# An unread identity matmul in every step of layer 1, and one head-sum per two steps in layer 0, in a two-layer graph attention kernel

## What is computed

```python
# layer 0 (transformer): K[src], Q[dst], V[src]
score = einsum('ehd,ehd->eh', K[src], Q[dst]) / sqrt(32) + edge_bias
ex = exp(score - segment_max(score, dst)[dst])
out = segment_sum(ex / segment_sum(ex, dst)[dst] * V[src], dst) @ Wp + bp   # then layer norms and an FFN
# layer 1 (GAT): feat = (h @ W_lin + b_lin) @ W_gat; el, er = sums of feat * attn_l, feat * attn_r per head
e = leaky_relu(el[src] + er[dst], 0.2)
out = segment_sum(softmax over dst of e * feat[src], dst)                   # then a bias, leaky_relu, h_in + out
```

## Time and profile before

| | us |
|---|---|
| median of 3 runs (5990.07 to 6003.05) | 5992.57 |
| the profiled execution | 5990.54 |
| its span, first to last instruction | 5988.6 |

### The profile page before, as it was taken

One profiled execution on the slowest core, in us unless ns is written; L12 is line 12 of the kernel. 1 busy time (PEld: TensorE's weight loads), 2 busy tenths in 40 slices (PEclk: granted clock), 3 DMA queues, 4 the chain that ended last, 5 costly groups with the idle time before them and its releaser, 6 DMA issues.

```text
span 5988.6 us, 127287 instructions
## 1 busy us (share of the span) xinstructions
PE 5460.7 (91%) x26094; PEld 4327.4 (72%) x26094; DVE 4924.3 (82%) x12464; ACT 3152.8 (53%) x10275; POOL 3747.5 (63%) x4022
## 2 busy tenths in 40 slices
PE   8978888888888888888999998999999999999988
PEld 5556666666666666667999996777777777777766
DVE  4469999999999999996777775887888788878864
ACT  3446666666566566643333334555555555655533
POOL 1147776666667666644444446777777777777733
PEclk9999999999999999999999997777777777767789
DMA  5668898888888888872222224777777777777767
GB/s 177 212 222 290 286 290 284 286 287 282 287 283 288 286 284 283 288 234 83 85 85 85 84 83 140 221 218 222 218 220 218 219 218 218 220 218 219 218 201 230
DMA packets 723026, 1313.61 MB, mean 219 GB/s; under 512 B 109088, under 2 KB 502132, under 8 KB 722421
## 3 DMA queue, kind: packets, MB, share of 16 engines
q0 software_dynamic: 200192, 634.41, 36.8%
q1 hardware_dynamic: 444802, 422.18, 23.4%
q10 hardware_dynamic: 77426, 250.73, 10.9%
HBM read 964.16 MB, written 342.73 MB: 218 GB/s over the span
## 4 chain that ended last, share of the span: by engine, by line
PE 37%; DVE 30%; issue 18%; POOL 5%; DMA 4%; DVEq 3%; SPq 2%; ACT 2%; POOLq 1%; ACTq 0%
PE bank L816 35%; DVE sred L1199 7%; DVE prod L1193 7%; DVE ev L1284 5%; DVE acc L1299 4%; POOL Gf L525 3%; DMA Gf<-ft_tab,srcs 3%; PE bank L819 2%; POOL Gf L576 1%; DVE U L1251 1%; DVE Y L1252 1%; DVE scan L1261 1%; DVEq L1181 1%; DVEq L1284 1%; DVE scan L1239 1%
## 5 line engine op out<-in xcount | busy, mean ns | idle before, releaser
L816 PE MATMUL bank<-ev,oh 128*128 128x264 f32 x7040 | 2310.6, 459 | 88.7 <-DVE ev L1284 88.0
L525 POOL DMA_INDIRECT Gf<-kv_tab,srcs x1564 | 1570.4, 1004 | 724.1 <-issue 480.1
L525 POOL DMA_INDIRECT Gf<-ft_tab,srcs x1564 | 1598.9, 1022 | 483.2 <-issue 401.8
L816 PEld LDWEIGHTS bank<-ev,oh 128*128 128x128 f32 x7040 | 1480.0, 223 | 346.0 <-DVE ev L1284 123.4
L816 PE MATMUL bank<-Gf 128*128 128x128 f32 (+3 forms) x6480 | 1263.8, 346 | 22.1 <-ACT Gf L805 15.6
L1284 DVE TENSOR_TENSOR ev<-Gf,ex 128x528 f32<-128x528 f32 x1760 | 1232.9, 701 | 2.1 <-ACT ex L688 1.4
L816 PE MATMUL bank<-qs,oht 128*128 128x256 f32 x3520 | 954.8, 394 | 226.9 <-DVE prod L1193 226.6
L816 PEld LDWEIGHTS bank<-Gf 128*128 128x128 f32 x6480 | 967.2, 192 | 221.0 <-issue 98.5
L621 ACT ACTIVATE absd<-lane,dlocs 128x128 f32<-128x128 f32 x3520 | 1112.9, 389 | 4.0 <-DVE bms L1166 3.5
L816 PEld LDWEIGHTS bank<-qs,oht 128*128 128x128 f32 x3520 | 599.5, 190 | 437.6 <-issue 371.8
L1299 DVE SCALAR_TENSOR_TENSOR acc<-acc,same,bank 128x264 f32<-128x264 f32 x1540 | 736.0, 478 | 34.2 <-PE bank L816 30.8
(11 more groups left out here) (160 smaller groups left out, 6183.6 us busy)
## 6 DMA issues: line engine op xcount, KB each, us to landing
sums<-acc ACTq DMA_DIRECT2D x440, 528.0 KB
qs<-q_tab SPq DMA_DIRECT2D x880, 128.0 KB
qs<-dst_tab SPq DMA_DIRECT2D x880, 128.0 KB
Gf<-sums SPq DMA_DIRECT2D x196, 132.0 KB, 2.1
kv_tab<-Gf SPq DMA_DIRECT2D x98, 260.0 KB, 2.1
Gf<-in_x SPq DMA_DIRECT2D x196, 128.0 KB, 2.1
Gf<-kv_tab,srcs POOLq DMA_INDIRECT x1564
Gf<-ft_tab,srcs POOLq DMA_INDIRECT x1564
```

Of the source, the lines that this page charges most:

```text
L525: pool.indirect_dma_start(out=rows[layer][:, m % SLOTS[layer], k, :], out_offset=None, in_=tab, in_offset=bass.IndirectOffsetOnAxis(ap=src ...
L816: return nc.tensor.matmul(o, a, r, start=first, stop=end)
```

## The change

**Layer 1:** TensorE multiplies `ident` (128 by 128) by `w_l[:, 0, :]` (256 columns) into bank 0 once in each of the 880 steps, between `spread` and `agg`. Nothing waits for it and nothing reads it.

**Layer 0:** `prod` gets four places instead of two. `reduce` runs in odd steps only and sums the products of two steps in one instruction over 1024 numbers instead of two over 512; `scores` waits for four of them. In an even step nothing stands in its place.

```diff
-        prod = sb("prod", [P, 2, 2, D])
+        prod = sb("prod", [P, 4, 2, D])
...
+            def unread():
+
+                mm(bank[0][:, 0:D], ident[:, :], w_l[:, 0, :])
...
                         if C.live:
                             spread(layer, C, r)
+                        if layer == 1 and B.live:
+                            unread()
                         C, r = step_at(B, s - 12)
...
-                V.tensor_tensor(prod[:, s % 2, :, :], step_rows(0, at)[:, :, 0:D],
+                V.tensor_tensor(prod[:, s % 4, :, :], step_rows(0, at)[:, :, 0:D],
...
             def reduce(B, s):
+
+                a = s - 1
                 dve.wait_ge(E_["prodd"], B.c * ST + s + 1)
-                V.tensor_reduce(hc(sred[:, :])[:, :, 2 * s:2 * s + 2].rearrange("p h c -> p c h"),
-                                prod[:, s % 2, :, :].rearrange("p k (h w) -> p k h w", h=H), AXX,
+                V.tensor_reduce(hc(sred[:, :])[:, :, 2 * a:2 * a + 4].rearrange("p h c -> p c h"),
+                                prod[:, a % 4:a % 4 + 2, :, :].rearrange("p a k (h w) -> p (a k) h w", h=H), AXX,
                                 ALU.add).then_inc(E_["redd"], 1)
...
-                    dve.wait_ge(E_["redd"], B.c * ST + ST)
+                    dve.wait_ge(E_["redd"], (B.c + 1) * ST // 2)
...
-                            if layer == 0:
+                            if layer == 0 and s % 2 == 1:
                                 reduce(B, s)
-                            elif s == 7:
+                            elif layer == 1 and s == 7:
                                 leaky(B)
```

More of the change, by code:

```diff
@@ L269, in build @@
         ohs = [v[:, k * SPAN:(k + 1) * SPAN] for v in (oht[:, :, :, :].rearrange("p a k n -> p (a k n)"),
-                                                       prod[:, :, :, :].rearrange("p a k n -> p (a k n)")) for k in range(4)]
+                                                       prod[:, 0:2, :, :].rearrange("p a k n -> p (a k n)")) for k in range(4)]
         dloc, lk, bm = [v[:, :, :].rearrange("p (b s) k -> p b (s k)", s=ST) for v in (dlocs, lks, bms)]
```

## The result

| | median us | runs | from | to |
|---|---|---|---|---|
| before | 5997.70 | 10 | 5990.07 | 6006.09 |
| after | 6021.09 | 10 | 6003.97 | 6028.74 |

The ratio after to before is 1.0035, with a 95% interval of 1.0024 to 1.0047: slower by 0.35%, some 21 us (23 between the medians), and more than the 0.2% that a measurement of this kernel can tell. The forecast was 5948 us, 45 us faster; the time lies 35 us above the upper end of the range, on the other side of zero.

A forecast was written before the change was run, and what follows sets the result against it. VectorE was taken to bound layer 0's edges and GpSimd's back-to-back gathers layer 1's. Layer 0 -29, layer 1 -15 and tail -1 gave -45 us, from 5992.6 to 5948 us, range 5890 to 5986.

The forecast's parts named there:

- Layer 1, the bound: Layer 1's edges: GpSimd issues gathers back to back and sets the pace, not the busier TensorE; stage 2068 us.
- The added matmul and the clock: Layer 1: a step takes 1.94 us at full clock, clock rises above 0.9, work hidden within 2.36 us a step.
- Layer 1, -15 us: Layer 1: slightly shorter gathers, as slow stretches with VectorE in step with GpSimd go: -15 us.
- The merged sum's price: Layer 0: 440 fixed costs of 0.065 us go by merging sums: 29 us gained, 22 to 35 at the ends.
- What gets late in front of L1269: Layer 0, step 2: cover for TensorE's transpose falls to 0.19 us; if the semaphore takes that, up to 11 us return.
- The step that failed: Layer 0's edges: VectorE is full, so each microsecond off its queue shortens the span until another engine is late.
- (3): Rival, layer 1: clock does not rise and the added matmul lands on half clock, +229 us, total 6190; chance 0.05.
- (4): Rival, layer 1: gathers lengthen with `ev` locked onto their starts, +60 to +142 us, total 6050; chance 0.04.
- Rival (2): Layer 1 gives 0, layer 0 only 0 to -10 (merged sum slower per number or L1269 waits): 5987 us; chance 0.08.
- The signs of being wrong: Layer 1 gap before a gather above 0.3 us, mean gather changed by over 0.03 us, or clock below 0.81.
- The tail, -1 us: End of the span: VectorE's last L1215 comes 0.34 us late because of TensorE in a slow stretch: -1 us.

The follow-up runs named there:

- e1: The kernel before with only the unread matmul added in layer 1: 5997.69 us, ratio 0.9996.
- f3: The kernel after, with GpSimd in layer 0 waiting for the landing three spans back instead of two: 5967.73 us, ratio 0.9947.
- f1: The kernel before, sums unpaired, with GpSimd in layer 0 waiting for the landing three spans back instead of two: 5992.76 us, ratio 0.9985.
- e8: e2 with GpSimd in layer 0 waiting for the landing three spans back instead of two: 5966.29 us, ratio 0.9953.
- e5: The kernel after without the unread matmul, each odd step of layer 0 making two sums over 512 instead of one long one: 6025.82 us, ratio 1.0048.
- e2: The kernel after without the unread matmul, so only layer 0's paired sums against before: 6014.25 us, ratio 1.003.
- f2: e5 with GpSimd in layer 0 waiting for the landing three spans back instead of two: 5991.37 us, ratio 0.9992.
- e4: e3 with the unread matmul added in layer 1, ahead of `spread`: 5905.53 us, ratio 0.9852.
- e3: The kernel before with layer 1's `ex` in PSUM bank 0, leaving `ev` one SBUF operand: 5983.5 us, ratio 0.9974.
- e11: Same code as f1, run on another chip where the kernel before took 7333 us: 7337.2 us, ratio there 1.0018.

## Why the prediction was wrong, by its own steps

**Layer 1, the bound: right.** "The busiest engine is not the bound if the one that feeds it is never held up": GpSimd has no gap above 0.3 us in 3900 to 5700 us in after either, and the clock's rise from 0.72 to 0.97 left the median where it was (e1).

**The added matmul and the clock: right, with a price a little low.** A step takes 1.88 us at full clock (4601.42 to 4603.30 in after). The forecast was 1.94, but 0.16 of that was for the chain, of which this step has nothing; the matmul holds 0.52 us here (4601.89 to 4602.41) and not 0.44. Both fit into the 2.36 us of a step:

```profile
4601.42 0.61 PE L816 MATMUL bank<-erq,prod 128*128 128x8 f32 x4
4601.89 0.68 PE L816 MATMUL bank<-steps,ident 128*128 128x256 f32 x2
4602.41 1.05 PE L816 MATMUL bank<-ev,oh 128*128 128x264 f32 x4
4603.30 0.51 PE L816 MATMUL bank<-erq,prod 128*128 128x8 f32 x4
```

**Layer 1, -15 us: didn't come.** The mean gather went from 1.022 to 1.028 us, and the stage is 8.5 us longer. That is a loss neither: six other kernels whose layer 1 is that of before have means of 1.021 to 1.026 us and stages of 2072.5 to 2079.3, and f3, with the matmul, 1.023 and 2074.5. e1's interval, 0.9986 to 1.0006, leaves no room for 15 us. With TensorE out of the way VectorE waits for rows instead; why gathers still meet `ev` as often was not looked into. This is a term that was sized wrong, and too small to make the forecast fail.

**The merged sum's price: right.** Held 1.13 us against twice 0.596; 26.3 us over the layer, forecast 29 with 22 at the low end. The Trainium skill, VectorE: DVE Perf Modes, in its section on the errata of SBUF sources, gives the formula from which the estimate of 27 us was made; its longer fixed term, which would have given 69, fits neither this row nor the 16-wide one.

**What gets late in front of L1269: right.** L1277, its name in after, shows no idle time in 600 to 2400 us of layer 0; the 0.19 us of slack were enough.

**The step that failed** is in the first part: "each microsecond taken from VectorE's queue in layer 0 is one of the span, until another engine is late". I never worked out how late the next engine was. I took GpSimd's waits for VectorE as proof of room: an engine that sets the pace doesn't wait for others. But the same view of the kernel before has two more lines, which I passed over:

```profile
POOL Gf L525 <- issue: 362.9, 947, 3.8
POOL Gf L525 <- DVE ev L1284: 140.1, 148, 4.2
POOL Gf L525 <- DMA Gf<-kv_tab,srcs: 62.1, 136, 1.9
```

Less 0.30 us for each gap, these are 96 us of waiting for VectorE (140.1 - 148 x 0.30), 79 without a named releaser (362.9 - 947 x 0.30) and 21 that end with a landing (62.1 - 136 x 0.30). Only the first are surely room; behind a landing GpSimd has stood at its own `LAND` wait, with rows still to be fetched. f1 shows how much of it that was: with LAND 3 in the order of before the 21 are gone, the 79 are 48 (319.4 - 903 x 0.30), and GpSimd waits 183 us for VectorE in place of 96. And the room isn't where it is needed. In the steps 3 to 7 of a block VectorE has few extras, and a step takes 0.60 + 0.62 + 0.60 + 0.40 = 2.22 us (the two in the middle from the earlier trace rows, `product` and `add` as medians of the layer). GpSimd, without any wait, takes 1.78 x (1.004 + 0.30) = 2.32. So even before, VectorE gained on it there by 0.10 us a step, and lived on the rows in the ring. In after it is 2.22 - 0.03 = 2.19 against 1.78 x (1.041 + 0.30) = 2.39, 0.20 a step, twice as much, and rows run out at the end of a block, where the waits behind `scores` stand.

These are estimates, and they leave out the wait that decides. In e8 the same sum gives 1.78 x (1.074 + 0.30) = 2.45 us for GpSimd, a wider gap than in after, and no row is late. What the runs show in the place of the failed step is this: layer 0 has a second limit, the rows that GpSimd delivers while it stops at the landing two spans back, and it lay just under VectorE's queue. Moving the sums raised it over it (e5, stage +36 us with VectorE's work unchanged), and looking three spans back lowers it again (e2 to e8, 2302.6 to 2255.4 us), after which the merged sum's gain comes through.

**The second omission** is that the prediction asked about `ev` and gathers in layer 1 and not in layer 0, where the change moves VectorE's whole order. There the mean gather went up by 0.037 us, 57 us over the layer, more than the gain. That alone is not the loss, since at LAND 3 gathers of 1.07 us cost next to nothing (f2 against f1). The working says of layer 0 that "VectorE has 0.6 us less and in an odd one as much more" and checks only TensorE against it.

**The rivals.** None of them was what happened. The two slower ones were placed in layer 1: (3) the clock, which rose, and (4) gathers that get longer by `ev`: they do, but in layer 0, and what that costs there hangs on LAND, which no rival had. Rival (2) had the right result for layer 1 and a wrong reason for layer 0. The slower side got 0.09 in all, because layer 0 was held to have one answer.

**The signs of being wrong** that the prediction named didn't show: in layer 1 no gap before a gather exceeds 0.3 us, the mean gather moved by 0.006 us, and the clock is 0.97. All three watched layer 1. Of layer 0 it said only what it should gain, 22 to 35 us, and the stage became 33.6 us longer.

**The tail, -1 us:** the ends of the span gave -1 us in all; this can't be told from other things that moved.

## What to carry to other kernels

Before booking a microsecond taken from the fullest engine, work out the margin of the engine that feeds it, in that stage and in the part of the loop where the consumer is fastest, its own waits included. Count a supplier's wait as room only if the consumer ends it, not if its own transfers do. Moving work in one queue moves when it meets another engine's accesses, so an edit that only regroups instructions has to be checked against every engine that its operands can hold up. A faster clock or a freed engine that gives nothing may give much once its feeder is faster: try it again behind each change of the bound (worth 0 us in e1, 78 us in e4).

## What the hardware showed that was not expected

- A VectorE operation with two SBUF operands holds up an indirect DMA that GpSimd starts under it until the operation gives way, also through two in a row (1.79 us for 0.95). `ev` with an operand in PSUM doesn't: 0.956 us in the mean in e3 in place of 1.022. Nor does the sum, with one operand (0.947 us over 229 gathers in after). But `members`, which has one tensor operand too, adds 0.08 us in the mean to the 139 gathers of layer 1 that start under its writing of `prod` in e4.
- In layer 0 the place where GpSimd waits for the landing of its own transfers matters more than how long its instructions take: from e2 to e8 gathers became longer, 1.038 to 1.074 us, and the stage shorter, 2302.6 to 2255.4.
- Two unread records of 256 columns a step lifted the clock of layer 1 from 0.72 to 0.97 while TensorE's busy share fell from 94% to 90%.
- On one chip the same kernel took 7333 us in place of 5998, with VectorE's `product` at 679 ns as elsewhere and, in e11, 911 us of VectorE's idle time without a named releaser.
